# A causal attention kernel in which GpSimd's additions of probabilities are cut into instructions of at most 512 columns

## The reference

```python
scores = jnp.einsum('bhki,bhqi->bhkq', k, q) / math.sqrt(HEAD)
mask = jnp.arange(n)[:, None] <= jnp.arange(n)[None, :]
scores = jnp.where(mask, scores, jnp.float32(-10000.0))
attn = jax.nn.softmax(scores, axis=2)
combined = jnp.einsum('bhkq,bhkl->bhql', attn, v)
out = combined.transpose(0, 2, 1, 3).reshape(b, n, HIDDEN)
x = _layernorm(x + out @ W_out + b_out)
...
x = _layernorm(x + mixture_of_depths_ffn(x))
```

## Time and profile before

| What | Value |
|---|---|
| median of three runs | 2638.15 us (2637.4 to 2640.35) |
| the profiled execution, its own time | 2636.7 us |
| its span in the trace | 2634.9 us |
| PE busy | 2526.2 us, 96% |
| DVE busy | 1737.9 us, 66% |
| POOL busy | 1518.8 us, 58% |
| ACT busy | 1230.9 us, 47% |
| POOL's additions (L732) | 704.3 us to or from Pm, 349.3 us from P3; 496 instructions |
| share of the chain that ended last | PE 81%, DVE 6%, ACT 4%, POOL 3% |

### The profile page before, as it was taken

One profiled execution on the slowest core, in us unless ns is written; L12 is line 12 of the kernel. 1 busy time (PEld: TensorE's weight loads), 2 busy tenths in 40 slices (PEclk: granted clock), 3 DMA queues, 4 the chain that ended last, 5 costly groups with the idle time before them and its releaser, 6 DMA issues.

```text
span 2634.9 us, 40165 instructions
## 1 busy us (share of the span) xinstructions
PE 2526.2 (96%) x13920; PEld 1810.5 (69%) x13920; DVE 1737.9 (66%) x4224; ACT 1230.9 (47%) x2342; POOL 1518.8 (58%) x1229
## 2 busy tenths in 40 slices
PE   5999999999999999999999999998899999999997
PEld 4566666666666666666667666665588888888885
DVE  5757678777777877777787677777465435643532
ACT  1555565566565566665565665565631111111110
POOL 0566787687788777778777777876331213122311
PEclk8999999999999999999999999998999999999998
DMA  6766557676666767656666575764431011001000
GB/s 172 127 113 127 101 129 161 125 156 138 137 137 124 164 134 149 154 113 145 126 162 144 124 167 116 141 135 129 160 102 36 25 33 41 17 25 41 29 20 16
DMA packets 167931, 289.57 MB, mean 110 GB/s; under 512 B 23153, under 2 KB 58033, under 8 KB 166578
## 3 DMA queue, kind: packets, MB, share of 16 engines
q1 hardware_dynamic: 160562, 270.15, 47.4%
q0 software_dynamic: 7168, 16.85, 2.0%
HBM read 120.11 MB, written 65.11 MB: 70 GB/s over the span
## 4 chain that ended last, share of the span: by engine, by line
PE 81%; DVE 6%; ACT 4%; POOL 3%; DMA 3%; issue 2%; SPq 1%; ACTq 0%; DVEq 0%; POOLq 0%
PE PS L1385 13%; PE PS L1368 13%; PE PS L1238 10%; PE PS L1318 10%; PE PS L1334 9%; PE PS L1287 9%; PE PS L1252 7%; PE PS L1246 7%; POOL Pa L732 3%; PE PS L1261 2%; DVE xTl L1046 2%; DMA Qp<-nat 1%; DMA h_s<-hs 1%; DVE nm L948 1%; ACT Pm L851 1%
## 5 line engine op out<-in xcount | busy, mean ns | idle before, releaser
L732 POOL TENSOR_TENSOR Pa<-Pa,Pm 128x1024 f32<-128x1024 f32 (+2 forms) x332 | 704.3, 2137 | 168.7 <-ACT Pm L851 119.3
L1318 PE MATMUL PS<-Qp,Kp 98*128 98x512 f32 (+3 forms) x1536 | 548.0, 361 | 16.3 <-ACT P L851 4.6
L851 ACT ACTIVATE Pm<-PS 128x512 f32<-128x512 f32 (+3 forms) x856 | 397.1, 471 | 336.0 <-PE PS L1318 319.7
L1287 PE MATMUL PS<-Kp,Qp 96*128 96x512 f32 (+3 forms) x1536 | 503.9, 363 | 37.8 <-DMA Qp<-nat 18.2
L948 DVE TENSOR_REDUCE nm<-PS 128x1 f32<-128x512 f32 x512 | 345.5, 686 | 223.8 <-PE PS L1287 223.2
L1318 PEld LDWEIGHTS PS<-Qp,Kp 98*128 98x128 f32 x1536 | 293.0, 192 | 220.8 <-ACT Pm L851 92.8
L732 POOL TENSOR_TENSOR Pa<-Pa,P 128x1024 f32<-128x1024 f32 (+2 forms) x164 | 349.3, 2145 | 78.6 <-ACT P L851 55.4
L1287 PEld LDWEIGHTS PS<-Kp,Qp 96*128 96x128 f32 x1536 | 284.0, 194 | 117.3 <-issue 32.5
L820 ACT ACTIVATE G<-PS,b1c 128x512 f32<-128x512 f32 x128 | 88.2, 689 | 539.6 <-PE PS L1368 520.6
L956 DVE CUSTOM_DVE_ANT_0 PS<-PS,maskA 128x384 f32<-128x384 f32 (+3 forms) x512 | 245.3, 505 | 143.5 <-PE PS L1287 141.8
L1385 PE MATMUL PS<-W2h,Gs 128*128 128x512 f32 x1024 | 316.6, 390 | 0.9 <-DVE W2l L1051 0.9
(11 more groups left out here) (139 smaller groups left out, 4343.8 us busy)
## 6 DMA issues: line engine op xcount, KB each, us to landing
Kp<-nat SPq DMA_DIRECT2D x192, 256.0 KB, 6.1
Qp<-nat SPq DMA_DIRECT2D x192, 256.0 KB, 6.6
x_raw<-in_xt SPq DMA_DIRECT2D x16, 1024.0 KB, 6.1
o_s<-Of SPq DMA_DIRECT2D x64, 256.0 KB, 2.1
Ot<-o_s SPq DMA_DIRECT2D x64, 256.0 KB
xb<-in_x SPq DMA_DIRECT2D x64, 256.0 KB, 3.5
h_s<-hs SPq DMA_DIRECT2D x64, 256.0 KB, 3.7
out<-xb SPq DMA_DIRECT2D x64, 256.0 KB, 3.6
```

Source lines behind the costliest of these rows:

```text
L732: e.tensor_tensor(to, to, tile[:, h0:h0 + many, 0:w], ALU.add).then_inc(s["padd"], many // 2)
L851: e.activation(probs(u, k)[:, h_, 0:w], PS[:, B_BANKS[j % 2], 0:w], ACT.Exp).then_inc(s["b_exp"], 1)
L1287: ins = e.matmul(to, Qp[0:96, u % 4, h_, qt * P:qt * P + P], Kp[0:96, (2 * i + k0 // 512) % 4, h_, 0:w], start=True, stop=True)
L1318: e.matmul(PS[:, B_BANKS[j % 2], 0:w], Kp[0:98, (2 * i + k // 4) % 4, h_, k % 4 * P:k % 4 * P + P], Qp[0:98, u % 4, h_, 512 - w:512], star ...
```

## The change

An addition for a step of 512 or 384 columns a head is issued as four instructions of one head each, where there were two of two heads; for a step of 256 or 128 columns it is two instructions of two heads, where there was one of four. So 496 instructions become 992, and what is added stays the same. The semaphore padd now counts 4 for a step, where it counted 2; the three waits on it are rescaled and wait for the same steps as before.

```diff
--- before.py
+++ after.py
@@ -722,14 +722,14 @@
                     if a is not None and not by_products(u):
                         if i is not None:
                             e.wait_ge(s["keep"], i + 1)
-                        e.wait_ge(s["padd"], 2 * a)
+                        e.wait_ge(s["padd"], 4 * a)
                         if k == 1:
                             e.wait_ge(s["pv"], ksteps_before(u) + 1)
                         w = width(u, k)
-                        many = 2 if w > 256 else 4
+                        many = 1 if w > 256 else 2
                         for h0 in range(0, HG, many):
                             to = acc[:, u % 2, h0:h0 + many, 512 - w:512]
-                            e.tensor_tensor(to, to, tile[:, h0:h0 + many, 0:w], ALU.add).then_inc(s["padd"], many // 2)
+                            e.tensor_tensor(to, to, tile[:, h0:h0 + many, 0:w], ALU.add).then_inc(s["padd"], many)
                 for j in o_beat.get(n - 1, ()):
                     o = o_number(j)
                     k = o % 2
@@ -843,7 +843,7 @@
                             u0, k0 = [(x_, y_) for x_ in (u - 1, u) for y_ in range(8) if added(x_, y_) == a - 3][0]
                             if not by_products(u0):
                                 e.wait_ge(s["pv"], ksteps_before(u0) + k0 + 1)
-                                e.wait_ge(s["padd"], 2 * (a - 2))
+                                e.wait_ge(s["padd"], 4 * (a - 2))
                             elif k0 == ksteps(u0) - 1:
                                 e.wait_ge(*done(("N", u0)))
                             else:
@@ -1203,7 +1203,7 @@
                 elif kind == "N":
                     u = job[1]
                     if not by_products(u):
-                        e.wait_ge(s["padd"], 2 * added_before(u + 1))
+                        e.wait_ge(s["padd"], 4 * added_before(u + 1))
                 elif kind == "C":
                     e.wait_ge(s["wo_in"], 16)
                     e.wait_ge(s["bias"], 16)
```

## The result

The changed kernel takes 2661.78 us (median of four runs, 2655.85 to 2665.96), the kernel before beside it 2638.0 (2637.4 to 2640.35): ratio 1.0103, 95% interval 1.0082 to 1.0123. A second comparison gave 2660.38 against 2633.58, 1.0104 (1.0078 to 1.0129). So it is slower, by 24 to 27 us in the medians where the forecast had 10. (A ratio is given here with its interval as it is on record; it is not the quotient of the two medians, which is 1.0090 for the first.) The profiled execution of the change is its longest, 2665.96, with a span of 2664.2.

The account below looks back on a forecast made before the run. PE bounds the kernel, busy 96%, with about zero slack against POOL at step 7's mask in plain pairs. Terms 22 + 4 - 9 - 7 + 1 = +11 us gave 2649, rounded to 2648 us; range 2624 to 2665.

Parts of the forecast that it names:

- The price of an instruction, 0.13: On POOL, each further addition instruction costs 0.13 us, with 0.10 and 0.16 as ends.
- DVE's relief wins: Rival: in split pairs, DVE's shorter waits outweigh POOL's added instructions, making the kernel faster, 2625 us; chance 0.22.
- Plain pairs, +22: In 20 pairs without a DVE input split, POOL's last mask comes 1.1 us later, all paid by PE: +22 us.
- Early units, +4: In units 1, 3 and 7, PE already waits for the last mask; 1.4 us more each, +4 us.
- -3 for a DMA's wait: First split after the start: PE's wait for a DMA of Q, started by DVE's late result, shrinks: -3 us.
- Unit 5 is held by other things and is left at zero: In early unit 5, longer POOL work was taken to add nothing: zero us.
- Clock in the early units: Unit 7 comes to waits like those behind which the clock fell in unit 3: +1 us.
- Split pairs, -9: In six pairs where DVE splits an input, PE's waits for DVE mostly go: 12.6 saved, 3.4 lost to clock, -9 us.
- L956 elsewhere, -4.5: PE's waits for DVE's L956 outside the split pairs' odd units go nearly whole: -4.5 us.
- that saves 2.1 in each: In each of six split pairs, PE's waits for DVE mostly go and POOL's 28.8 us stays: 2.1 us saved.
- the one on the clock: Rival: in plain pairs the clock also falls behind PE's 1.1 us wait, 34 us more, 2681 us; chance 0.08.

Follow-up runs that it names:

- e8: Kernel before's additions, but steps 2 to 5 of the 20 plain odd units cut into eight half-head instructions each: 2717.83 us, ratio 1.0317 to the kernel before.
- e5: The changed kernel with additions split only in the odd units of the 20 plain pairs: 2657.06 us, ratio 1.0092 to the kernel before.
- e1: The changed kernel with the mask of step 7 issued ahead of the additions of step 6 in odd units: 2625.01 us, ratio 0.9955 to the kernel before.
- e13: The changed kernel with units 0 to 7 as before, in addition size and semaphore increments: 2653.66 us, ratio 1.0073 to the kernel before.
- e11: The change, units 0 to 7 and from 60 whole, step 7's mask moved ahead, and step 5's in split pairs: 2615.95 us, 0.993 of the kernel before.

## Why the prediction was right in sign and wrong in size

- **The price of an instruction, 0.13: right.** From start to start a piece of 1024 columns takes 2351 ns in the median, one of 512 takes 1244, one of 256 takes 693 (e8): 137 and 142 ns for each cut. The estimate of 60 ns worked out from the Trainium skill's page GPSIMD Engine Reference, section Elementwise, does not hold here. The page's 2.6 cycles are rounded, and with 2.63 next to nothing would be left of its 4497 ns, so its figures give no such price. With the measured price fell the rival *DVE's relief wins*.
- **Plain pairs, +22: right.** Measured +21.7 in the table, +1.03 in the window. The products of steps 6 and 7 start 1.50 apart for 0.48 before: a wait of 0.87, and the 0.15 by which they had overlapped. e5 shows it alone, e1 shows that the mask's place is the cause.
- **Early units, +4, with +1 for the clock and -3 for a DMA's wait: wrong, and the largest miss.** +2 was forecast there and +9.2 measured. Two steps failed. The first is *Unit 5 is held by other things and is left at zero*. PE's waits for masks in units 0 to 8 grew from 5.2 to 12.5: by 1.1, 1.3 and 1.4 in units 1, 3 and 7, nearly the 4 of the forecast, but also by 3.6 in unit 5, where 0.62 became 1.56 and 2.62. With the DMA's 2.5 gone as forecast, and 1.5 of other waits, PE's idle time there grew from 11.6 and 11.9 us to 15.0 and 15.1, by 3.3. The second is *Clock in the early units*. The time at 0.50 doubled from 17.1 to 34.1 us in both profiles, and the 5.9 us that are left of the 9.2 go with it, where I had put 1. I had asked whether the clock would fall in one more unit; it fell at all four, for 6.8 or 10.2 us, where it had stood low for 6.8 behind unit 1, 3.4 (6.8 in the second profile) behind unit 3, 3.4 behind unit 5, and not at all behind unit 7. e13, which takes the splitting there back, has 17.1 and 224.9 again.
- **Split pairs, -9, and L956 elsewhere, -4.5: too large.** Measured -6.7, and nothing to be seen outside the split pairs: the waits for L956 in plain pairs are in one profile of the kernel before, while the other has 11.3 us in seven waits, none of it in plain pairs. The step that failed in the split pairs is *that saves 2.1 in each*: I let PE meet POOL again at step 7 alone. It also meets it at step 5, where up to 2.1 us of the old waits came back as a wait for the mask. PE's idle time in the six pairs together fell by 3.6 only, from 19.8 and 21.9 to 18.1 and 16.4, where 2.1 in each would be 12.6; the clock fell in four and five of the six, where I had put two. e11 shows that this mask held 0.9 of a pair's time; that the sums and exponentials hold the rest is read from the waits that came in there, and no run takes those away.
- **Sum.** Early +7 and the gains of DVE +7 too good make 14 of the 14 to 17 us between the forecast's +10 and the two comparisons. The time lies inside the range; of the rivals the one on the clock was nearest in its effect, but in the early units and not in the plain pairs.

## What to carry to other kernels

Before an engine's work is cut finer for the sake of a neighbour, look for the one place where a third engine waits for the end of that work; at next to no slack every cut is paid there nearly in full (9 cuts of 0.14 us a unit, less 0.1 to 0.2 of room, made 21.7 us in 20 units here), and the neighbour's shorter waits return only what the next one in line lets through (31 to 37 us less on DVE's split gave PE 7). Putting the awaited instruction ahead of the work that no one waits for paid with either granularity (0.9975 with whole additions; 0.9955 with split ones, which have 1.0104 without it). Where PE already waits, cost a longer wait at its length and again for the time that the clock then stands low.

## What had not been expected of the hardware

- Around PE's waits of 2.5 to 2.6 us for a mask in the early units the clock stood at 0.50 for 6.83 or 10.24 us. Around 0.85 to 0.99 us in the plain pairs of the change it stayed at 1.00 in 39 of 40.
- Two profiles of one kernel differ by 3.1 us (before) and 4.1 us (the change) in the "rest", as much as the change makes there (+2.9); only the second profile of both kernels showed that.
